# Key norms in a decoder layer's cross-attention: a quadratic form for half of the heads

## What is computed

```python
q = (hidden_states @ Wq).reshape(B, Sq, H, D)          # H = 16, D = 128
k = (encoder_hidden_states @ Wk).reshape(B, Skv, H, D)  # 1500 keys a batch
v = (encoder_hidden_states @ Wv).reshape(B, Skv, H, D)
q = rmsnorm(q, gq)
k = rmsnorm(k, gk)   # x * rsqrt(mean(x * x) + 1e-5) * g
scores = jnp.einsum('bqhd,bkhd->bhqk', q, k) * scale
attn = jax.nn.softmax(scores, axis=-1)
out = jnp.einsum('bhqk,bkhd->bqhd', attn, v).reshape(B, Sq, H * D) @ Wo
```

## Time and profile before

| | us |
|---|---|
| runs of the kernel, median of 3 | 1323.64 (1322.04 to 1323.68) |
| profiled execution, span from the first to the last instruction | 1321.1 |
| own time of the profiled execution | not recorded apart from its span; the runs lie 0.9 to 2.6 above that span |
| PE, DVE, ACT, POOL busy in the span | 1290.7, 1155.3, 1074.3, 1089.0 |
| phase -1 (keys of batch 0 alone) | from 153.35 to 189.16 |
| one half of a phase, 12 steps, in the middle | 33.56 and 32.93 |

### The profile page before, as it was taken

The page is one execution under the profiler, slowest core; times in us unless marked ns, Lnnn a source line. Parts: engine busy times, 40 slices in busy tenths (PEclk is TensorE's granted clock), DMA queues, the critical chain, the costliest instruction groups (busy, mean ns, idle before and its releaser), DMA issues.

```text
span 1321.1 us, 21768 instructions
## 1 busy us (share of the span) xinstructions
PE 1290.7 (98%) x6516; PEld 1059.3 (80%) x6516; DVE 1155.3 (87%) x1777; ACT 1074.3 (81%) x3171; POOL 1089.0 (82%) x922
## 2 busy tenths in 40 slices
PE   8989999999999999999999999999999999999998
PEld 5767677788888888888888888888888888878787
DVE  5866689999999999999999999999999999997755
ACT  2667788899999999999999999999899999973442
POOL 5644452989999999999999999999999999999840
PEclk9989999999999999999999999999999999999999
DMA  7140230101010101010101010101010101030300
GB/s 254 46 160 1 80 136 13 36 13 36 13 36 12 36 12 36 13 36 13 36 13 36 13 36 13 35 13 36 13 36 10 38 9 40 1 112 1 115 24 29
DMA packets 27845, 54.12 MB, mean 41 GB/s; under 512 B 2816, under 2 KB 22400, under 8 KB 25936
## 3 DMA queue, kind: packets, MB, share of 16 engines
q1 hardware_dynamic: 26736, 52.38, 11.8%
q10 hardware_dynamic: 992, 0.36, 0.1%
HBM read 44.60 MB, written 8.13 MB: 40 GB/s over the span
## 4 chain that ended last, share of the span: by engine, by line
PE 83%; ACT 5%; DVE 5%; POOL 4%; issue 3%; ACTq 0%; POOLq 0%; DVEq 0%
PE xa_k_ps L1419 12%; PE xa_k_ps L1420 11%; PE xa_k_ps L1421 11%; PE xa_s_ps L1420 5%; PE xa_s_ps L1421 5%; PE xa_s_ps L1419 5%; PE xa_o_ps L1419 5%; PE xa_o_ps L1421 4%; PE xa_o_ps L1420 4%; PE om_ps L1516 3%; PE xa_o_ps L1510 3%; PE xq_ps L634 2%; POOL xa_den L1170 1%; POOL probs_r L1184 1%; DVE xa_ss L1349 1%
## 5 line engine op out<-in xcount | busy, mean ns | idle before, releaser
L1349 DVE TENSOR_REDUCE xa_ss<-xa_sq 125x6 f32<-125x768 f32 x360 | 339.5, 943 | 3.7 <-ACT xa_sq L1267 2.2
L1184 POOL TENSOR_TENSOR probs_r<-probs,xa_p_hi 125x896 fp32r<-125x896 f32 (+1 forms) x160 | 330.4, 2065 | 5.3
L1419 PE MATMUL xa_k_ps<-wk_parts,xa_ctxT_hi 128*125 128x512 f32 x768 | 324.0, 422 | 6.2 <-ACT xa_sq L1267 5.9
L1420 PE MATMUL xa_k_ps<-wk_parts,xa_ctxT_hi 128*125 128x512 f32 x768 | 302.8, 394 | 0.0
L1421 PE MATMUL xa_k_ps<-wk_parts,ctxT_lo 128*125 128x512 f32 x768 | 302.4, 394 | 0.0
L1336 DVE TENSOR_TENSOR xa_scores<-xa_s_ps,xa_rk 125x448 f32<-125x448 f32 x384 | 237.8, 619 | 50.8 <-PE xa_s_ps L1421 48.4
L1170 POOL TENSOR_TENSOR xa_den<-probs,xa_den 125x896 f32<-125x896 f32 x128 | 272.8, 2131 | 3.7 <-ACT probs L1248 3.7
L1226 ACT ACTIVATE xa_sq<-xa_k_ps 125x512 f32<-125x512 f32 x360 | 213.8, 594 | 26.0 <-DVE xa_ss L1349 16.6
L1248 ACT ACTIVATE probs<-xa_scores 125x896 f32<-125x896 f32 x192 | 182.8, 952 | 57.0 <-POOL xa_scores L1159 35.1
L1266 ACT ACTIVATE xa_k_ps<-xa_k_ps 125x128 f32<-125x128 f32 x720 | 193.9, 270 | 21.6 <-PE xa_k_ps L1421 21.3
L1357 DVE TENSOR_TENSOR xa_max_ps<-xa_scores,xa_max_ps 125x448 f32<-125x448 f32 x320 | 198.1, 619 | 0.6
(11 more groups left out here) (187 smaller groups left out, 2479.1 us busy)
## 6 DMA issues: line engine op xcount, KB each, us to landing
xa_ctx_nat<-in_ctx SPq DMA_DIRECT2D x16, 750.0 KB
ctxT_in<-in_ctxT SPq DMA_DIRECT2D x84, 125.0 KB, 2.1
qo<-in_xo_w SPq DMA_DIRECT2D x1, 2048.0 KB, 16.7
qo<-in_xq_w SPq DMA_DIRECT2D x1, 2048.0 KB, 15.3
vo_scratch<-qo SPq DMA_DIRECT2D x2, 1024.0 KB, 4.0
w_parts_scratch<-ws_hi SPq DMA_DIRECT2D x2, 1024.0 KB, 4.1
w_parts_scratch<-ws_lo SPq DMA_DIRECT2D x2, 1024.0 KB, 5.3
vo<-vo_scratch SPq DMA_DIRECT2D x1, 2048.0 KB, 8.8
```

The lines of the kernel that those rows point to most:

```text
L1184: pool.tensor_tensor(probs_r[0:KP, slots, :], probs[0:KP, slots, :], p_hi[:, y // 2 % (NPR // 2), first:2, :].bitcast(F32), ALU.subtract). ...
L1349: dve.tensor_reduce(ss[:, i // 2, UH * (i % 2):UH * (i % 2) + vector_heads(of)], squares(of, i).rearrange("p (g d) -> p g d", d=XD), AX.X, ...
L1419: pe.matmul(out, l_hi, r_hi, start=first, stop=False)
L1420: pe.matmul(out, l_hi, r_lo, start=False, stop=False)
```

## The change

For the first 4 heads of each group of 8 (heads 0 to 3 and 8 to 11, `GH = 4`), the sum of the squares of k = Wk' c is computed as c' G c with G = Wk Wk' of 128 by 128. G is made on chip by eight 128 by 128 matmuls in `query_path` (`gram`), and takes the place of these heads' Wk in the columns of `wk_hi` and `wk_lo`. Bank 0 of a step then holds c G for 4 heads. It is made with two matmuls instead of three: with c = h + l, it is h G, and DVE multiplies it with m = 2c - h and sums it over the 128 columns. So each step has four tensor_tensor_reduce on DVE (L1404 of the changed kernel), and no square of bank 0 and no TENSOR_REDUCE. Bank 1 keeps its three matmuls, and all 4 of its heads go through ACT's square with the accumulator (L1307). m is made from a third copy of the context: SP loads it in three parts a batch (`load_m`), ACT rounds a part (`round_m`, 512 columns), DVE doubles and subtracts (`double_m`, L1367, 512 columns). The mean's factor goes into the reductions.

```diff
-WH = 6
+GH = 4
+MT = 4
+M_HI_AT = {3: (0, 2), 11: (1, 0), 19: (1, 1)}
+M_AT = {6: (0, 2), 14: (1, 0), 22: (1, 1)}
...
+            def gram(i):
+
+                pe.wait_ge(qn_ready, V - 3 if i == 0 else V)
+                for g in range(QH):
+                    head = wkT[:, GRAM_HEADS[i] + g, :]
+                    mm = pe.matmul(ps[:, GRAM_BANKS[i], g * C:(g + 1) * C], head, head, start=True, stop=True)
+                mm.then_inc(gram_mm, 1)
...
+            def load_m(ph, part):
+
+                wait(sp, formed, ph.at(STEPS, 2 * MT * (part + 1)) if ph.b >= 0 else 0)
+                src = a.ctx[ph.b + 1].rearrange("(p t) c -> p t c", t=KT)
+                sp.dma_start(m_tiles(part), src[:, MT * part:MT * (part + 1), :]).then_inc(m_loaded[part], 16)
...
+            def round_m(ph, part):
+
+                act.wait_ge(m_loaded[part], 16 * (ph.b + 2))
+                wait(act, m_ready, m_count(ph, part) - 1)
+                act.activation(m_hi[:, :, :], m_tiles(part), ACT.Copy).then_inc(m_hi_ready, 1)
...
-                        wait(act, summed, ph.at(STEPS, STEPS + j - 1))
-                        act.activation(squares(ph, j)[:, 0:4 * XD], k_ps[0:KP, (2 * j) % 3, :], ACT.Square
-                                       ).then_inc(squared, 1)
...
-                        for g in range(own, 4):
-                            head = UH * (j % 2) + 4 + g
+                        for g in range(UH - GH):
+                            head = UH * (j % 2) + GH + g
                             cols = k_ps[0:KP, (2 * j + 1) % 3, g * XD:(g + 1) * XD]
-                            act.activation(cols, cols, ACT.Square, accum_out=ss[:, j // 2, head:head + 1])
-                        act.activation(squares(ph, j)[:, 4 * XD:(4 + own) * XD],
-                                       k_ps[0:KP, (2 * j + 1) % 3, 0:own * XD], ACT.Square).then_inc(squared, 1)
+                            last = act.activation(cols, cols, ACT.Square, scale=MEAN ** 0.5,
+                                                  accum_out=ss[:, j // 2, head:head + 1])
+                        last.then_inc(squared, 1)
...
+            def double_m(ph, part):
+
+                dve.wait_ge(m_hi_ready, m_count(ph, part))
+                dve.scalar_tensor_tensor(m_tiles(part), m_tiles(part), 2.0, m_hi[:, :, :].bitcast(F32),
+                                         ALU.mult, ALU.subtract).then_inc(m_ready, 1)
...
-                        dve.wait_ge(squared, ph.at(2 * STEPS, 2 * STEPS + 2 * j))
-                        dve.tensor_reduce(ss[:, i // 2, UH * (i % 2):UH * (i % 2) + vector_heads(of)],
-                                          squares(of, i).rearrange("p (g d) -> p g d", d=XD), AX.X, ALU.add
-                                          ).then_inc(summed, 1)
+                        dve.wait_ge(k_done, ph.at(2 * STEPS, 2 * STEPS + 2 * j + 1))
+                        for g in range(GH):
+                            cols = k_ps[0:KP, (2 * j) % 3, g * C:(g + 1) * C]
+                            head = UH * (j % 2) + g
+                            form = dve.tensor_tensor_reduce(cols, cols, ctx_m[:, j // 2, :], MEAN, 0.0, ALU.mult, ALU.add,
+                                                            ss[:, j // 2, head:head + 1])
+                        form.then_inc(formed, 1)
...
-                return three(k_ps[0:KP, (2 * j + c) % 3, :], ctxT_hi[:, i, t, :], ctxT_lo[:, i, t, :],
-                             wk_hi[:, cols], wk_lo[:, cols])
+                out = k_ps[0:KP, (2 * j + c) % 3, :]
+                if c == 0:
+                    pe.matmul(out, ctxT_hi[:, i, t, :], wk_hi[:, cols], start=True, stop=False)
+                    return pe.matmul(out, ctxT_hi[:, i, t, :], wk_lo[:, cols], start=False, stop=True)
+                return three(out, ctxT_hi[:, i, t, :], ctxT_lo[:, i, t, :], wk_hi[:, cols], wk_lo[:, cols])
...
-                        wait(pe, squared, ph.at(2 * STEPS, 2 * STEPS + 2 * j - 2))
+                        wait(pe, squared, ph.at(STEPS, STEPS + j - 1))
                         project_k(ph, j, 0).then_inc(k_done, 1)
...
-                        wait(pe, squared, ph.at(2 * STEPS, 2 * STEPS + 2 * j - 1))
+                        wait(pe, formed, ph.at(STEPS, STEPS + j))
                         project_k(ph, j, 1).then_inc(k_done, 1)
```

More of the change, by code:

```diff
@@ L930, in early_products, with m_part @@
     return [divmod(i, XH) for i in range(first, last)]
-def vector_heads(ph):
-    return UH if ph.b == -1 else WH
+def m_part(at, ph, j):
+    if j not in at:
+        return None
+    ahead, part = at[j]
+    to = ph.shift(ahead)
+    return (to, part) if to.within(0, B - 2) else None
 def split_at(ph, j):
@@ L1015, in probs_pair, with m_tiles, m_count @@
             return probs[0:KP, y % NPR:y % NPR + 2, :]
[L1017 to L1021, removed]
+        def m_tiles(part):
+            return ctx_m[:, MT * part:MT * (part + 1), :]
+        def m_count(ph, part):
+            return KT // MT * (ph.b + 1) + part + 1
         wk_hi_ready, wk_lo_ready, ones_set = (
@@ L1028, in cross_attention @@
         qhi_ready, qlo_ready = sem("xa_qhi_ready"), sem("xa_qlo_ready")
-        k_done, squared, summed = sem("xa_k_done"), sem("xa_squared"), sem("xa_summed")
+        k_done, squared, formed = sem("xa_k_done"), sem("xa_squared"), sem("xa_formed")
+        m_loaded = [sem(f"xa_m_loaded{i}") for i in range(KT // MT)]
+        m_hi_ready, m_ready = sem("xa_m_hi_ready"), sem("xa_m_ready")
         mean_ready, ln_ready, table_ready, rk_ready = (
@@ L1078, in body @@
                         load_part(ph, c)
+                    load_m(ph.shift(1), 2)
+                if ph.b == -1:
+                    for part in range(KT // MT):
+                        load_m(Phase(0), part)
+                        if part < 2:
+                            mlp.store_parts(sp, part)
                 if ph.b == B - 1:
@@ L1090, in body @@
                     mlp.load_w2(sp)
-                if ph.b == -1:
-                    mlp.store_parts(sp)
             attention.sync(sp)
             query.sync(sp)
+            for part in range(KT // MT):
+                load_m(Phase(-1), part)
             sp.dma_start(ident_in, a.ident).then_inc(ident_loaded, 16)
@@ L1291, in beside @@
             def beside(c):
+                if c in (-6, -4, -2):
+                    round_m(Phase(-1), (c + 6) // 2)
                 if 0 <= c < 4:
-                    if c == 0:
+                    part = slice(c * 512, (c + 1) * 512)
+                    if c % 2 == 0:
+                        act.wait_ge(query.gram_mm, c // 2 + 1)
+                        act.activation(wk_hi[:, part], query.gram_ps(c // 2), ACT.Copy).then_inc(wk_hi_ready, 1)
+                    else:
                         act.wait_ge(wk_loaded, 16)
-                    part = slice(c * 512, (c + 1) * 512)
-                    act.activation(wk_hi[:, part], wk_in[:, part], ACT.Copy).then_inc(wk_hi_ready, 1)
+                        act.activation(wk_hi[:, part], wk_in[:, part], ACT.Copy).then_inc(wk_hi_ready, 1)
                 if c == 4:
@@ L1399, in beside @@
             def beside(c):
+                if c in (-5, -3, -1):
+                    double_m(Phase(-1), (c + 5) // 2)
                 if 1 <= c <= 4:
@@ L1636, in load_raw, with store_parts @@
                      ).then_inc(self.wraw_loaded[1], 16)
[L1638 to L1643 removed]
+    def store_parts(self, sp, i):
+        sp.wait_ge(self.whi_made, 4 * (i + 1))
+        sp.dma_start(self.a.w_parts[2 * i], self.whi[:, :].bitcast(F32)).then_inc(self.whi_stored, 16)
+        sp.wait_ge(self.wlo_made, 4 * (i + 1))
+        sp.dma_start(self.a.w_parts[2 * i + 1], self.wlo[i][:, :].bitcast(F32)).then_inc(self.wlo_stored, 16)
     def split_weights(self, pool, m):
```

55 lines of the change are left out of this document (31 added, 24 removed).

## The result

| | before | after |
|---|---|---|
| median of 4 runs | 1323.66 us | 1375.63 us |
| lowest to highest | 1322.04 to 1323.95 | 1374.61 to 1376.14 |
| span of the profiled execution | 1321.1 | 1372.8 |

The ratio is 1.0393, 95% interval 1.0379 to 1.0408. The forecast was 1396, in a range of 1286 to 1470. The sign came true, and DVE is the full engine as forecast. The size was 20 us too high, as the difference of larger errors: the pair is cheaper than forecast, and most of the slow-down is a wait that the forecast had left to a rival. The profiled execution of after took 1374.61 us for its span of 1372.8, so an execution holds 1.8 us outside its span, not the 2.5 given above.

A forecast was written before the change was run, and what follows sets the result against it. PE bounds the kernel before (66.2 of 66.5 us a phase), and DVE would take over at 71.4. +74 - 4 + 2 = +72 on the span of 1321.1 gives 1393, plus 2.5 makes 1396 us, range 1286 to 1470.

The forecast's parts named there:

- the pair: On DVE, one product with sum over 128 columns plus the row writing the sum out; 96 a phase, 0.29 us each.
- the 2.5 given above: Whole kernel: the runs' median was put 2.5 us above the profiled execution's span, turning 1393 into 1396.
- p = 0.29: DVE's time in us for one product and its reading; 96 a phase gave 27.8 and DVE 71.4 us a phase.
- the reading: The short DVE row after each product that writes the sum out; put at 0.09 to 0.14 us.
- Product alone: On DVE, one 128-column product from PSUM with a reading that costs nothing: 0.20 us from start to start.
- Rival 1: On DVE, the reading hides in the gap after each product: p 0.20 to 0.22, around 1290 us; chance 0.25.
- the other -2: Outside phases 0 to 14: -4 us in phase -1 and +2 for the matmuls making G.
- The doubling at 0.6 each: On DVE, three 512-column doublings a phase with both operands in SBUF, some 0.6 us each, 1.8 a phase.
- Rival 3: DVE's doubling waits for the POOL instruction under way: half of 6.3 us a phase, +47, so 1443; chance 0.10.
- 41.8: DVE's us a phase once the reduction goes (62.4 - 20.6), before doublings (1.8, making 43.6) and products are added.
- +74: Phases 0 to 14: DVE needs 4.9 us a phase more than now, in place of PE, over 15 phases.
- -4 and +2 for G: Phase -1: 24 steps shorter by 0.15 us each, -4; eight matmuls for G and the first split's wait, +2.

The follow-up runs named there:

- e3: The changed kernel with the third matmul put back in bank 0, so the context's low part times G counts twice; 1393.09 us, ratio 1.0526 to before.
- e12: The changed kernel without the doubling on DVE and with the third matmul back in bank 0, nothing left out; 1345.70 us, ratio 1.0169 to before.
- e2: The changed kernel with the doubling's second operand a broadcast column in PSUM in phases 0 to 14, same size and place; 1337.05 us, ratio 1.0104 to before.
- e1: The changed kernel without the doubling on DVE, so m is the context itself; 1320.16 us, ratio 0.9976 to before.
- e6: The changed kernel with three heads a tile on DVE, the fourth computed as k and squared by ACT in the same bank; 1383.17 us, ratio 1.0457.
- e10: e1 with the first score maximum of each half phase copied by ACT instead of a product on DVE; 1318.57 us, ratio 0.9962 to before.

## Why the prediction was right, and where its terms were not

1. **DVE becomes the bound and PE's saving is lost under it.** Right: DVE has 69.2 of 69.9 us, two gaps of 0.2 for PE, and PE waits before the first matmul of bank 1 for L1404, 4.8 us a phase where I had said 5. ACT at 57.9 (58.4) and POOL at 63.7 (63.0) are as summed. PE's busy time fell by 2.4 and not by 5.5: the first matmul of bank 1 now lasts 448 ns on average (L1479, below), where the earlier trace rows has 0.40; e3 and e12 say what the saving is worth, 1.1 and 1.6 us a phase.
2. **p = 0.29 was too high.** It is 0.247. The step that failed is the reading: I gave it 0.09 from the short rows (the next start comes 0.10 behind DVE's and 0.09 behind ACT's) and had 0.14 from ACT's surcharge, and it costs 0.04. Product alone, 0.20 in the text, is 0.21. This is 96 x 0.043 = 4.1 us a phase too much, 62 in all. Rival 1 had the overlap right, but for its condition p had to be below 0.239. With p = 0.247 the sum as it stands is right: DVE needs 43.6 + 23.7 = 67.3, 0.8 more than 66.5, so 12 over 15 phases and, with the other -2, 1334 us. e2, which has this pair and a doubling that doesn't wait, took 1337.
3. **The doubling at 0.6 each was too low.** Rival 3 was true, not an alternative to the forecast: 4.8 us a phase instead of 1.8, +3.0 or 45 in all. It had been priced at +47 with a chance of 0.10; e2, which removes only the waiting, gives back 38.6. The Trainium skill ("SBUF — State Buffer", section "SBUF: two separate sides") says that a VectorE instruction with two SBUF inputs and a GpSimd instruction that reads SBUF exclude each other; by that rule the traces agree, with 0.68 us for 512 columns when one operand is in PSUM and up to 2.39 when both are in SBUF.
4. **The rest of DVE's sum.** 41.8 + 23.7 + 4.8 = 70.3, and a phase in the middle takes 69.86, 0.4 less: -7 over 15 phases. The first and the last of the 15 grow by less than the middle ones (3.24 on average where those have 3.37): -2. So +74 - 62 + 45 - 7 - 2 = +48, the measured 48.6 but for rounding.
The groups behind points 1 and 2, from the page of after (busy, mean ns, idle before):

```profile
L1404 DVE CUSTOM_DVE_ANT_0 xa_k_ps<-xa_k_ps,xa_ctx_m 125x128 f32<-125x128 f32 x1536 | 399.2, 325 | 8.5 <-PE xa_k_ps L1491 8.4
L1479 PE MATMUL xa_k_ps<-wk_parts,xa_ctxT_hi 128*125 128x512 f32 x384 | 172.2, 448 | 73.2 <-DVE xa_ss L1404 70.7
L1404 DVE DVE_READ_ACCUMULATOR2_ANT xa_ss<- 125x1 f32 x1536 | 224.5, 146 | 0.0
```

5. **Phase -1: -4 and +2 for G were wrong.** It is +3.9. PE starts the projections 1.7 us later, and its 24 steps take 38.1 us instead of 35.8. By the sums (PE, DVE and ACT at 1.15 to 1.24 a step) it should have been shorter, and no engine is full in it now (27.6 of 30.0 for PE). What it waits for, us and times in 160 to 190:

```profile
DVE xa_k_ps L1404 <- PE xa_k_ps L1491: 7.7, 17, 1.7
POOL ws_hi L1716 <- DMA w_parts_scratch<-ws_hi: 5.2, 1, 5.2
PEld xa_k_ps L1490 <- ACT xa_k_ps L1307: 4.5, 12, 0.6
...
PEld xa_k_ps L1479 <- DVE xa_ss L1404: 3.9, 14, 0.6
ACT xa_k_ps L1307 <- PE xa_k_ps L1481: 3.3, 9, 1.3
```

PE waits for DVE and ACT, and both for PE: the banks of k go round and the sums no longer tell. e1 and e3 have it as well (192.7 and 195.3 for the first maximum), and e6 more. That it is the number of banks was not tested, so the cause of these 3.9 us stays open.

That the forecast came near is luck, two errors against each other: had the doubling not waited, as in e2, it would have been 59 us too high. The condition that it gave for itself, p of 0.27 to 0.33, didn't hold. What the runs support is this account: forms and matmul alone -3.5 us (e1 against before), the work of the doubling +16.9 (e2 against e1), its waiting for GpSimd +38.6 (after against e2), +52.0 together.

## What to carry to other kernels

Before an elementwise step goes to VectorE beside a busy GpSimd, look where its operands lie: one operand in PSUM made this one 0.68 us long at every place, and with both in SBUF it took up to 2.4. A rival that is a cost on top of the forecast, and not in place of it, belongs in the sum with its chance. And once three engines stand within 3 us of each other in a phase of 66, work taken from the fullest one can give nothing (e10: 1.0 us of work, 0 of time): look then at what the next engines wait for, and not at the fullest one's sum alone.
